# Sine products before the swap of halves, the swap as an accumulating transfer, and a new order of work in a step

## The reference

```python
q = _silu(x @ Wq)                       # k, v alike; z = x @ Wz
q = _causal_dwconv(q, conv_q_w)         # 4 taps along the tokens; k, v alike
def rot_half(u):
    u1, u2 = jnp.split(u, 2, axis=-1)
    return jnp.concatenate([-u2, u1], axis=-1)
q = q * cos + rot_half(q) * sin
k = k * cos + rot_half(k) * sin
q = q / max(norm(q), 1e-12)             # k alike
for s in range(4):                      # four lags
    attn = einsum('bshd,bshd->bsh', q, lag(k, s)) / sqrt(D)
    out += (attn * sigmoid(lag(a, s) * b))[..., None] * lag(v, s)
out = out * rsqrt(mean(out * out) + 1e-6) * norm_w * _silu(z)   # then @ Wout
```

## Time and profile before

| | us |
|---|---|
| median of 3 runs (1355.78 to 1356.19) | 1356.13 |
| profiled execution, its own time | 1355.53 |
| its span, first to last instruction | 1353.7 |
| DVE busy | 982.0 |
| ACT busy | 784.5 |
| POOL busy | 485.1 |

### The profile page before, as it was taken

One profiled execution on the slowest core, in us unless ns is written; L12 is line 12 of the kernel. 1 busy time (PEld: TensorE's weight loads), 2 busy tenths in 40 slices (PEclk: granted clock), 3 DMA queues, 4 the chain that ended last, 5 costly groups with the idle time before them and its releaser, 6 DMA issues. The chain is left out here.

```text
span 1353.7 us, 22528 instructions
## 1 busy us (share of the span) xinstructions
PE 1318.3 (97%) x6568; PEld 1103.8 (82%) x6568; DVE 982.0 (73%) x1531; ACT 784.5 (58%) x1504; POOL 485.1 (36%) x634
## 2 busy tenths in 40 slices
PE   6999999999999999999999999999999999999998
PEld 5688888888888888888888888887888888888886
DVE  7889999999999999999999999996122223334342
ACT  5666676767766666666666676766543444422221
POOL 6245454545545455555555454553000000000001
PEclk9999999999999999999999999999999999999999
DMA  8366656666566566665666656555710101156543
GB/s 262 81 131 127 134 116 151 133 130 136 120 146 135 124 132 134 140 141 121 130 144 121 147 119 139 123 118 137 243 40 24 47 15 55 50 184 203 170 133 139
DMA packets 141562, 171.83 MB, mean 127 GB/s; under 512 B 32720, under 2 KB 69584, under 8 KB 141264
## 3 DMA queue, kind: packets, MB, share of 16 engines
q1 hardware_dynamic: 114160, 121.48, 32.0%
q0 software_dynamic: 27360, 49.82, 21.6%
HBM read 62.58 MB, written 25.30 MB: 65 GB/s over the span
## 5 line engine op out<-in xcount | busy, mean ns | idle before, releaser
L1254 DVE TENSOR_TENSOR hid_lo<-relu,hid_hi 128x512 fp32r<-128x512 f32 x64 | 44.3, 692 | 169.1 <-ACT hid_hi L1246 169.1
L798 DVE SCALAR_TENSOR_TENSOR y_k<-u_k,cw_k,y_k 128x512 f32<-128x512 f32 x192 | 146.1, 761 | 27.4 <-ACT y_k L651 20.6
L798 DVE SCALAR_TENSOR_TENSOR y_q<-u_q,cw_q,y_q 128x512 f32<-128x512 f32 x192 | 144.4, 752 | 22.5 <-ACT y_q L651 14.8
L1346 POOL TENSOR_TENSOR g_buf<-g_buf,up_raw 128x512 f32<-128x512 f32 x3 | 3.8, 1279 | 356.2 <-DVE g_buf L1406 356.2
L510 POOL TENSOR_TENSOR rnorm<-norms,neg_half 128x8 f32<-128x8 f32 x64 | 122.6, 1915 | 9.5 <-POOL norms L506 8.5
L1242 ACT ACTIVATE relu<-bank,us_sb 128x512 f32<-128x512 f32 x64 | 44.1, 690 | 123.3 <-PE bank L1265 123.3
L540 POOL DMA_DIRECT2D sq_sum<-out_sq x62 | 53.9, 869 | 162.4 <-DVE norms L831 112.4
L1366 ACT ACTIVATE hid_hi<-o_raw 128x512 fp32r<-128x512 f32 x64 | 40.2, 630 | 116.0 <-PE bank L1475 97.3
L1426 DVE TENSOR_TENSOR hid_lo<-o_raw,hid_hi 128x512 fp32r<-128x512 f32 x64 | 43.8, 690 | 79.9 <-ACT hid_hi L1366 79.9
L690 ACT ACTIVATE down_raw<-y_q 64x512 f32<-64x512 f32 x64 | 40.5, 632 | 103.3 <-PE bank L1036 103.3
L526 POOL TENSOR_TENSOR rq_win<-rq_win,const 128x32 f32<-128x32 f32 x64 | 30.1, 471 | 194.9 <-DMA rq_win<-rq_scratch 194.9
(11 more groups left out here) (193 smaller groups left out, 3711.8 us busy)
## 6 DMA issues: line engine op xcount, KB each, us to landing
swapped_q<-y_q SPq DMA_DIRECT2D x128, 128.0 KB, 2.4
swapped_k<-y_k SPq DMA_DIRECT2D x128, 128.0 KB, 2.4
o_scratch<-o_buf SPq DMA_DIRECT2D x64, 256.0 KB, 3.4
o_raw<-o_scratch SPq DMA_DIRECT2D x64, 256.0 KB, 4.0
down_raw<-down_raw POOLq DMA_DIRECT2D x63, 256.0 KB, 3.4
y_v<-down_raw POOLq DMA_DIRECT2D x63, 256.0 KB, 4.3
sq_sum<-out_sq POOLq DMA_DIRECT2D x62, 256.0 KB, 3.3
raw_q<-in_wq SPq DMA_DIRECT2D x16, 256.0 KB, 3.1
```

The lines of the kernel that those rows point to most:

```text
L798: nc.vector.scalar_tensor_tensor(y[n][:, g % 2, :], u[n][:, g % 2, i:i + CH], cw[n][:, bass.ds(h * TAPS + i, 1)], y[n][:, g % 2, :], ALU.m ...
L1254: nc.vector.tensor_tensor(hid_lo[:, j % HS, :], relu[:, j % 2, :], hid_hi[:, j % HS, :].bitcast(fp32), ALU.subtract).then_inc(hid_lo_done, 1)
```

## The change

The angle's sine is multiplied into y where y lies, and the swap and the sum are one accumulating transfer: `swapped = y * sin`, then POOL asks for `rot[0:64] += swapped[64:128]` and `rot[64:128] += swapped[0:64]`. The sine table's signs are exchanged, since the product is now made ahead of the swap. DVE has four rope instructions in a step where it had six; SP has none of the four swaps, POOL has four more transfers. `score` waits for the transfers (`rope_added`) where it waited for DVE's sums, and so does the end of ACT's part. The order of a step changes on DVE (k's rope is done one step later, between q's taps; `sum_fold`, `gate_scores` and `mask_band` stand between k's taps; `make_o` stands ahead of q's sine product), on ACT (`square_out` behind q's SiLU, both `squares` later, `silu_z` and `copy_v` ahead of the squares of k) and on POOL.

```diff
+    def wait_rope(eng, n, g, c):
+        wait(eng, rope_added[n][g % 2], 32 * (c // 2 + 1) if isinstance(c, int) else
+             c * 16 + (32 if g % 2 == 0 else 16))
...
     def on_sync(sp):
...
-            for n in "qk":
-                wait(sp, conv_done[n], 3 * c + 3)
-                wait(sp, rope_done[n], 3 * (c - 1))
-                for to, frm in ((0, HALF), (HALF, 0)):
-                    sp.dma_start(swapped[n][to:to + HALF, g % 2, :], y[n][frm:frm + HALF, g % 2, :]
-                                 ).then_inc(swap_in[n][g % 2], 16)
...
     def on_gpsimd(pool):
+        def add_swapped(n, g1, k):
+            wait(pool, rope_done[n], 2 * (k + 1))
+            pool.sem_inc(rope_asked, 1)
+            for to, frm in ((0, HALF), (HALF, 0)):
+                nc.gpsimd.dma_start(rot[n][to:to + HALF, cols(g1)], swapped[n][frm:frm + HALF, g1 % 2, :],
+                                    accum_op=ALU.add).then_inc(rope_added[n][g1 % 2], 16)
...
             if at := back(h, g, 1):
                 fold_squares(c)
                 add_last_tap(at[1], c)
+                add_swapped("q", at[1], c - 1)
+                add_swapped("k", at[1], c - 1)
             if at := back(h, g, 3):
                 make_gates(at[1], c - 3)
...
         schedule(pool, step)
+        for n in "qk":
+            add_swapped(n, G - 1, NC - 1)
         roots(H - 1, G - 1, NC)
...
     def on_vector(dve):
         def rope(n, i, g, c):
+            wait(dve, conv_done[n], 3 * c + 3)
             if i == 0:
-                wait(dve, conv_done[n], 3 * c + 3)
                 wait(dve, scores_done, c - 3)
-                op = nc.vector.tensor_tensor(to, y[n][:, g % 2, :], cos[:, cols(g)], ALU.mult)
-            elif i == 1:
-                wait(dve, swap_in[n][g % 2], 32 * (c // 2 + 1) if isinstance(c, int) else
-                     c * 16 + (32 if g % 2 == 0 else 16))
-                op = nc.vector.tensor_tensor(sw, sw, sin[:, cols(g)], ALU.mult)
+                op = nc.vector.tensor_tensor(rot[n][:, cols(g)], y[n][:, g % 2, :], cos[:, cols(g)], ALU.mult)
             else:
-                wait(dve, rope_done[n], 3 * c + 2)
-                op = nc.vector.tensor_tensor(to, to, sw, ALU.add)
+                if not (isinstance(c, int) and c < 2):
+                    wait_rope(dve, n, g, c - 2)
+                op = nc.vector.tensor_tensor(swapped[n][:, g % 2, :], y[n][:, g % 2, :], sin[:, cols(g)],
+                                             ALU.mult)
...
     def on_tensor(pe):
...
         def score(g2, k):
             ahead = 1 if g2 < G - 1 else 0
-            wait(pe, rope_done["q"], 3 * (k + 1 + ahead))
-            wait(pe, rope_done["k"], 3 * (k + 1))
+            wait_rope(pe, "k", g2, k)
+            wait_rope(pe, "q", g2, k)
+            if ahead:
+                wait_rope(pe, "q", g2 + 1, k + 1)
...
-    sin = np.concatenate([-np.sin(angle), np.sin(angle)], 0).astype(np.float32)
+    sin = np.concatenate([np.sin(angle), -np.sin(angle)], 0).astype(np.float32)
```

More of the change, by code:

```diff
@@ L297, in attention @@
     rope_done = {n: sem(f"rope_done_{n}") for n in "qk"}
-    swap_in = {n: [sem(f"swap_in_{n}{i}") for i in range(2)] for n in "qk"}
+    rope_asked = sem("rope_asked")
+    rope_added = {n: [sem(f"rope_added_{n}{i}") for i in range(2)] for n in "qk"}
     squares_done = sem("squares_done")
@@ L643, in silu_and_tap @@
             else:
-                wait(act, rope_done[n], 3 * (c - 1))
+                wait(act, rope_done[n], 2 * (c - 1))
             if g < G - 1:
@@ L703, in step @@
                 silu_and_tap("q", bank_qv, h, g, c)
+            if back(h, g, 4):
+                square_out(c - 4)
+            if not is_start(h, g):
                 silu_and_tap("k", bank_kz, h, g, c)
@@ L706, in step @@
                 split_hi("q", h + 1, c)
-            squares("q", g, c)
-            if back(h, g, 4):
-                square_out(c - 4)
             silu_and_tap("v", bank_qv, h, g, c)
@@ L712, in step @@
                 split_hi("k", h + 1, c)
[L713 to L719, removed]
+            squares("q", g, c)
             if at := back(h, g, 2):
@@ L730, in step @@
                 save_spill(at[1], c)
+            squares("k", g, c)
+            if g == 3 and not is_last(h):
+                split_hi("v", h + 1, c)
+            elif g == 3:
+                for n in "qkvz":
+                    act.wait_ge(wlo_done[n], H)
+                ffn.up_signs(0)
+                ffn.up_signs(1)
             if g == 1 and not (isinstance(h, int) and h == 0):
@@ L738, in on_scalar @@
         for n in "qk":
-            act.wait_ge(rope_done[n], 3 * NC)
+            act.wait_ge(rope_done[n], 2 * NC)
+            for i in range(2):
+                act.wait_ge(rope_added[n][i], 16 * NC)
         ffn.hidden(0, 0)
@@ L862, in step @@
             c = h * G + g
-            for n in "qk":
-                for i in (1, 2, 3):
-                    conv_tap(n, i, h, g, c)
+            at1, at3 = back(h, g, 1), back(h, g, 3)
+            conv_tap("q", 1, h, g, c)
+            if at1:
+                rope("k", 0, at1[1], c - 1)
+            conv_tap("q", 2, h, g, c)
+            if at1:
+                rope("k", 1, at1[1], c - 1)
+            conv_tap("q", 3, h, g, c)
+            conv_tap("k", 1, h, g, c)
+            if at1:
+                sum_fold(at1[1], c)
+            conv_tap("k", 2, h, g, c)
+            if at3:
+                gate_scores(at3[1], c - 3)
+                mask_band(at3[1], c - 3)
+            conv_tap("k", 3, h, g, c)
             if is_start(h, g):
@@ L883, in step @@
                         ALU.mult).then_inc(prod_done, 1)
[L884 to L889, removed]
+            if g == 3 and not is_last(h):
+                split_lo("q", h + 1)
+            conv_tap("v", 1, h, g, c)
             if is_start(h, g):
@@ L892, in step @@
             rope("q", 0, g, c)
[L893 to L896, removed]
             conv_tap("v", 2, h, g, c)
@@ L899, in step @@
                 conv_tap("v", 3, h, g, c)
+            if g == 3 and not is_last(h):
+                split_lo("k", h + 1)
+            if at3:
+                join_out(at3[1], c)
+                make_o(at3[0], at3[1], c - 3)
+            rope("q", 1, g, c)
+            if is_end(h, g):
                 dve.wait_ge(squares_done, NC)
@@ L902, in step @@
             if g == 3 and not is_last(h):
-                split_lo("k", h + 1)
                 split_lo("v", h + 1)
-            for i in (1, 2):
-                rope("q", i, g, c)
-                rope("k", i, g, c)
             if is_start(h, g - 1):
@@ L914, in step @@
                                             ).then_inc(gate_done, 1)
-            if at := back(h, g, 3):
-                join_out(at[1], c)
-                make_o(at[0], at[1], c - 3)
             if g == 1 and not (isinstance(h, int) and h == 0):
@@ L921, in on_vector @@
         schedule(dve, step)
+        rope("k", 0, G - 1, NC - 1)
+        rope("k", 1, G - 1, NC - 1)
         sum_fold(G - 1, NC)
```

1 line of the change is left out of this document (removed).

## The result

| | before | after |
|---|---|---|
| median, us (4 runs each) | 1355.95 (1353.48 to 1356.19) | 1376.59 (1376.07 to 1376.81) |
| span of the profiled execution | 1353.7 | 1374.6 |
| DVE busy | 982.0 | 887.2 |
| POOL busy | 485.1 | 665.0 |

After is 1.0156 times as long as before (95% interval 1.0138 to 1.0173): 20.6 us slower. DVE has 95 us less to do and POOL 180 us more, and PE, which sets the time, waits longer. This document calls the changed kernel *after*, and the kernel that it was made from *before*.

What follows compares the result with a forecast made beforehand. PE, busy 97%, was taken as the bound, so only its waits could be gained. From 1355.5 us: -11.7 (stalls at heads' ends), +36.6 (late gates), -3.6 (ACT's tail) gave 1376.8, so 1377; range 1339 to 1402.

Steps and rivals of the forecast that it cites:

- The issue: POOL's second k transfer of 64 partitions: 0.75 us, between half and whole price, so both issues end at 9.2.
- From the issues to the gates: POOL makes the gates behind k's issues: 9.2 + 0.1 + 1.34 = 10.65 us in the step.
- the short form: POOL's three make_gates instructions take 1.34 us, not the 2.07 beside a busy DVE, as DVE itself waits from 10.24.
- DVE's new order at no cost: DVE's coefficients ready at 11.68 in the step against 11.72 today: no gain or loss if gates come by 10.1.
- The window: q's transfers could delay the window's load on the DMA queues from 7.6 to about 9.1, costing 0 to 0.4 us.
- The stall that goes: PE's waits for coefficients, about one behind each head's end, vanish as DVE is relieved: -11.7 us, the gain's main term.
- The steps' loss: Late gates on POOL delay DVE's coefficients and PE by 0.6 us in each of 61 steps: +36.6 us.
- ACT's tail, -3.6: Last step: z's SiLU earlier on ACT removes PE's 2.1 us wait and 1.5 us of low clock; at worst 0.
- hidden: Rival 1: k's issues on POOL cost 0.6 or less each, gates at 10.1, PE loses nothing: 1341 us; chance 0.33.
- Whole price: Rival 2: 0.90 us an issue on POOL, 0.80 a step: 1390 us, to 1434 with slow gates; chance 0.25.
- The window late: Rival 3: accumulating transfers delay the window to 9.1 or beyond, 0.3 to 0.5 us a step: 1359 to 1371; chance 0.12.
- Nothing from DVE: Rival 4: the head's end still stalls as k's rope blocks q's taps, POOL hides: near 1353 us; chance 0.05.

Runs made afterwards that it cites:

- the run with the tap moved: After with DVE's second tap of k moved behind gate_scores and mask_band, POOL's order untouched: 1353.8 us, 0.9993 of before.
- the fastest kernel: After with POOL making the gates ahead of k's two transfers: 1340.45 us; with the tail's first make_gates also ahead of roots: 1339.31 us.
- three kernels that take 0.7 us or more out of the chain: After with gates ahead of k's issues, 1340.45 us; k's rope products ahead of q's first tap, 1340.69; one 128-partition issue for k, its swap omitted, 1340.37.

## Why the prediction was right, and where it was right by luck

Forecast 1377, measured 1376.6. The deciding mechanism was the forecast one, on nearly its own timetable. The sizes of several terms were not right, and their errors cancelled, so that the closeness of the two numbers is luck. To land in the stated range, 1339 to 1402, says little as well: it holds both signs, and the chance given to a slower kernel was 0.60.

**The timetable of the regular step** (us from q's projection):

| | forecast | after |
|---|---|---|
| k's sine product done | 7.11 | 7.13 |
| k's first issue starts | 7.69 | 7.71 |
| both issues done | 9.2 | 9.35 |
| gates done | 10.65 | 10.68 |
| coefficients masked | 12.23 | 12.26 |
| PE's load | some 12.3 | 12.31 |

- *The issue.* Taken as 0.75, measured as 0.82 by the rows and as 0.74 by what the second one costs the gates. The step put it nearer the whole price for a reason that held: the price hardly goes by size.
- *From the issues to the gates.* "9.2 + 0.1 + 1.34" is the step that failed, though its end is right. It has two errors. `rq_win` starts 0.57 before the issues' rows end (510.59 against 511.16), so less stands behind them than 1.44; the earlier trace rows had shown such an overlap, 0.25, for `norms` behind one issue. So `rq_win` starts at 8.78 in the step; the prediction's own sign asked for 9.2 or later, and 8.6 would have proved it wrong. And the short form was taken because DVE would be waiting. It is not: its second tap of k ends at 10.29, and `rq_own` takes 0.67 instead of 0.22 beside it. Without that, the gates come 0.88 after the issues and the step is at 13.66, as the run with the tap moved shows. So with the short form that the sum assumed (0.82 an issue, gates 0.88 behind) a regular step loses 0.03, not 0.6. The 0.44 us of `rq_own`, on top of the issues, are what made after slow in regular steps.
- *DVE's new order at no cost.* Right: with the gates early, the steps are 13.63.
- *The window.* Right: it cost nothing. It even came earlier. SP issues its load at 2.15 in the step (503.96), where it was 3.18 in before, and it lands after a median of 2.8 us, where it was 4.0, so q's transfers do not delay it.
- *The transfers fit.* Right: 37.3% + 21.9% of the DMA engines is 59.2% where it was 53.6%, and no wait of a regular step names one.

**The sum.** Forecast: -11.7 + 36.6 - 3.6 = +21.3. Measured: -16.0 + 37.2 + 0.2 - 0.4 = +20.9 (rounded to a tenth each).
- *The stall that goes* was sized by the list of waits, 11.7; by the steps' lengths it was 16.0. The list understates it, and it did so in after too (22.4 against 37.2).
- *The steps' loss* was sized as 61 equal ones of 0.6. It was 46 of 0.47 and 14 of 1.10. In the step shown PE's load is 0.51 later than its 11.80; the forecast had rounded 0.55 up for a window that was not late. Its sign of steps all alike, also behind a head's end, did not occur.
- *"So I take the 11.7 us of waits as gone"*: the old cause is gone, yet a stall of the same size stands there for another cause. The step behind a head's end, from 487.08:

```profile
490.57 0.68 DVE L824 TENSOR_TENSOR wlo_v<-raw_v,whi_v 128x512 fp32r<-128x512 f32 x1
...
491.87 0.75 DVE L813 SCALAR_TENSOR_TENSOR y_q<-u_q,cw_q,y_q 128x512 f32<-128x512 f32 x1 [0.61 <-ACT y_q L662]
...
495.06 1.64 POOL L559 DMA_DIRECT2D rot_k<-swapped_k  x2 [2.17 <-DVE swapped_k L836]
...
496.12 1.39 POOL L526 TENSOR_TENSOR rq_win<-rq_win,const 128x32 f32<-128x32 f32 x1
...
496.69 0.74 DVE L813 SCALAR_TENSOR_TENSOR y_k<-u_k,cw_k,y_k 128x512 f32<-128x512 f32 x1
...
497.59 0.22 POOL L529 TENSOR_TENSOR rq_own<-rq_win 128x16 f32<-128x16 f32 x1
```

  The third low part ends at 4.17 of the step, and DVE still waits 0.61 for ACT's y: the prediction's account of DVE holds (it put that end near 4.0). But q's first tap starts 0.28 later than in a regular step. Then `rq_win` is what meets the tap of k: it takes 1.39 instead of 0.85 and ends with the tap. Against the regular step, k's issues start 0.27 later (7.98 against 7.71), the gates are done 0.16 more behind them (3.13 against 2.97), and PE loads 0.16 more behind the mask's end: 0.6 in all, on top of the 0.5 of every step, is the 1.10. With the tap moved, the gates are done 2.60 behind k's first issue there and 2.52 in a regular step, so the meeting of the two costs 0.5 of the gates' time here too. Where the 0.27 and the 0.16 in front of PE's load come from, no run tells; the steps of the fastest kernel are 0.12 longer there as well.
- *ACT's tail, -3.6.* The wait on z's SiLU is gone and the granted clock stays at 1.00 there, both as forecast, and the step is 13.82 long where it was 15.07. It was given back behind: PE waits 1.8 for coefficients and 0.7 for `down_raw`. In after's last step:

```profile
946.16 1.76 POOL L559 DMA_DIRECT2D rot_q<-swapped_q  x2 [2.76 <-DVE swapped_q L836]
...
952.89 0.71 DVE L851 TENSOR_TENSOR coef<-bank,gates 128x528 f32<-128x528 f32 x1 [4.89 <-POOL gates L534]
953.05 0.69 ACT L1264 ACTIVATE relu<-bank,us_sb 128x512 f32<-128x512 f32 x1 [5.02 <-DMA rot_k<-swapped_k]
...
953.74 1.14 PE L1068 MATMUL bank<-rot_q,rot_k 128*128 128x132 f32 x8 [1.80 <-DVE coef L851]
```

  The last four issues stand ahead of `roots` and the gates there, and ACT waits 5.0 for the last transfer. The prediction named that second wait as the way to 0, and missed that the queue of its main term is in the tail too. That the same loss came when ACT's order was changed alone (a wait of 1.6 for coefficients in place of 2.1 for z) says that part of it needs no transfers: something else was next all along.

**The rivals.** The first, *hidden*, put its condition at an issue of 0.65 and its time at 1341. The condition doesn't follow from the prediction's own sum: at 0.55 us lost with 0.75, and 0.2 for each 0.1, nothing is lost only below about 0.48. Its chance of 0.33 was given with the looser condition. The time is the one of three kernels that take 0.7 us or more out of the chain (1340.4 to 1340.7), and even the corrected condition did not hold, since with an issue of 0.82 all but 0.03 was hidden in regular steps once the tap was out of the way. *Whole price* put an issue at 0.90, as near to the measured 0.82 as the forecast's 0.75, and had a wrong time, 1390, for it left the same overlap out. *The window late* did not occur. *Nothing from DVE*: the stall did stay, by another road.

## What to carry to other kernels

An engine that issues accumulating transfers executes its queue in order: place the issue behind whatever others wait for, and look when the thing that it asks for is made, before counting what the issue costs. When a step has a slack of 0.1 us, a short instruction that runs beside another engine's two-input one can decide the step: here it cost 0.44 us of every regular one. Line up the start times of both engines, instruction by instruction. And size a stall by the distance between equal events of the bottleneck engine, not by the sum of its listed waits.

## What was not expected of the hardware

- `rq_own`, a POOL instruction on small operands (128x16), takes 0.22 us alone and up to 0.69 beside a DVE instruction with two inputs. `rq_win` behind k's two issues takes 0.85 alone and 1.39 beside such an instruction. In the rows shown both end within 0.1 us of the end of DVE's instruction. Moving one DVE instruction changed the kernel by 22.8 us. The Trainium skill ("SBUF — State Buffer", section "Who interferes with whom") states that a DVE instruction with two inputs in SBUF contends with a GpSimd instruction that reads SBUF; these rows agree.
- An accumulating issue on POOL takes 0.82 us for 64 partitions of 512 numbers (half of a pair's 1.64) and 0.90 for 128. The next POOL instruction starts 0.57 before the end of the pair's rows, and 0.30 before the end of a single one (410.13 against 410.43).
- In before the granted clock was 0.69 in the stretch behind one wait of 2.1 us, and 0.50, the lower of its two levels (1.2 GHz), from 926 to 928. It stayed at 1.00 through waits of about 1 us, one in each head, and through a wait of 1.8 us in after's tail.
